# A decoder layer on one core: cross-attention's first maxima moved ahead of the residual work, mask probes and query splitting rearranged, key parts stored once

## The reference, cut to what matters

```python
x = x + self_attention(layernorm(x))        # 16 heads of 64, values rounded to fixed point
x = x + cross_attention(layernorm(x), ctx)  # 16 heads of 8, keys = values = ctx of 4 x 1601
x = x + mixture_of_experts(layernorm(x))    # 8 experts, 2 per token
```

## Time and profile before

| what | value |
|---|---|
| median of three runs | 664.87 us |
| the profiled execution | 664.56 us |
| its span in the trace | 662.8 us |
| busy in the span: TensorE, VectorE, ScalarE, POOL | 552.0, 496.2, 458.3, 140.1 us |
| granted TensorE clock, mean | 0.937 of full |
| bytes moved by DMA | 62.89 MB |

### The profile page before, as it was taken

The page is one execution under the profiler, slowest core; times in us unless marked ns, Lnnn a source line. Parts: engine busy times, 40 slices in busy tenths (PEclk is TensorE's granted clock), DMA queues, the critical chain, the costliest instruction groups (busy, mean ns, idle before and its releaser), DMA issues.

```text
span 662.8 us, 13915 instructions
## 1 busy us (share of the span) xinstructions
PE 552.0 (83%) x5115; PEld 303.4 (46%) x5115; DVE 496.2 (75%) x893; ACT 458.3 (69%) x815; POOL 140.1 (21%) x215
## 2 busy tenths in 40 slices
PE   5788897988777479989889998899989893899992
PEld 3455454545456233333333333233333232799992
DVE  3568889888986996888878887588878744576662
ACT  3888987898853046778678776577767873577750
POOL 5000001000003442230125010230001216222232
PEclk9999998999978779999999999699999987799995
DMA  9930953744766537010641018000000501111113
GB/s 227 251 115 6 194 214 107 160 153 138 217 155 194 89 112 243 2 52 1 144 133 51 2 40 205 32 1 2 2 2 4 191 6 51 40 41 42 42 29 103
DMA packets 31669, 62.89 MB, mean 95 GB/s; under 512 B 4526, under 2 KB 21338, under 8 KB 31156
## 3 DMA queue, kind: packets, MB, share of 16 engines
q0 software_dynamic: 8000, 40.91, 23.5%
q1 hardware_dynamic: 22020, 20.31, 10.5%
q10 hardware_dynamic: 1584, 0.79, 0.4%
HBM read 42.29 MB, written 19.30 MB: 93 GB/s over the span
## 4 chain that ended last, share of the span: by engine, by line
PE 45%; DVE 26%; issue 9%; ACT 9%; DMA 6%; SPq 2%; POOL 1%; DVEq 0%; POOLq 0%; ACTq 0%
DVE smax L1707 12%; PE pair L1102 11%; PE pair L1266 6%; PE pair L1077 6%; PE pair L1032 5%; DVE region_p L1570 4%; PE pair L1254 3%; ACT region_p L1346 3%; DVE region_p L1600 2%; ACT region_p L1434 2%; PE pair L930 2%; PE pair L1276 2%; PE pair L983 2%; DMA region_p<-nmT 1%; DMA region_b<-nmT 1%
## 5 line engine op out<-in xcount | busy, mean ns | idle before, releaser
L1434 ACT ACTIVATE region_p<-pair 128x1024 f32<-128x1024 f32 (+3 forms) x277 | 217.5, 811 | 70.9 <-PE pair L1077 65.5
L1707 DVE TENSOR_REDUCE smax<-pair 128x2 f32<-128x1024 f32 x192 | 225.7, 1219 | 48.5 <-PE pair L1032 47.6
L1570 DVE SCALAR_TENSOR_TENSOR region_p<-region_p 128x1024 int16<-128x1024 int16 (+1 forms) x56 | 68.2, 1219 | 9.8 <-ACT region_p L1332 7.8
L1102 PE MATMUL pair<-region_p,region_b 128*32 128x256 f32 (+1 forms) x832 | 68.7, 403 | 0.2 <-ACT region_p L1441 0.2
L1102 PE MATMUL pair<-region_p 128*32 128x256 f32 (+1 forms) x832 | 66.9, 395 | 0.5 <-ACT region_p L1441 0.4
L1077 PE MATMUL pair<-region_b,region_k 59*128 59x256 bf16 (+1 forms) x416 | 54.7, 273 | 8.5 <-ACT region_p L1434 3.9
L1032 PE MATMUL pair<-region_k,region_b 56*128 56x512 bf16 (+1 forms) x256 | 43.9, 360 | 15.5 <-DVE smax L1707 14.1
L1346 ACT ACTIVATE region_p<-region_p 128x256 f32<-128x256 int16 x128 | 51.6, 418 | 2.3 <-DVE region_p L1570 2.3
L1266 PE MATMUL pair<-region_p 128*128 128x128 f32 x368 | 45.7, 278 | 0.0
L1266 PEld LDWEIGHTS pair<-region_p 128*128 128x128 f32 x368 | 43.8, 195 | 0.0
L916 PE MATMUL pair<-identb,region_p 128*128 128x128 bf16 x256 | 20.6, 226 | 24.8 <-DVE region_p L1600 24.6
(11 more groups left out here) (249 smaller groups left out, 945.4 us busy)
## 6 DMA issues: line engine op xcount, KB each, us to landing
kimg<-region_k SPq DMA_DIRECT2D x56, 200.1 KB
region_k<-kimg POOLq DMA_DIRECT2D x8, 1400.9 KB, 16.7
region_b<-in_mask_Bx1xSxS_ff POOLq DMA_DIRECT2D x12, 800.5 KB, 6.9
region_p<-in_mask_Bx1xSxS_ff POOLq DMA_DIRECT2D x4, 800.5 KB, 13.1
region_k<-in_L_ffn_W POOLq DMA_DIRECT2D x3, 1024.0 KB, 8.4
xdisp<-region_x POOLq DMA_DIRECT2D x1, 2322.0 KB, 19.8
region_b<-in_ctx SPq DMA_DIRECT2D x3, 768.0 KB
xdisp<-region_x POOLq DMA_DIRECT2D x1, 2257.5 KB, 19.1
```

What stands on the lines that cost most here:

```text
L1102: last = pe.matmul(pair[3][32 * h:32 * h + 32, 512 + s % 2 * S:512 + (s % 2 + 1) * S], v_heads[b % 2][0:rows, t, c:c + 32], pT[0:rows, n / ...
L1434: act.activation(pT[0:rows, first // 3 % 2, k:k + size], home[0:rows, 0:size], ACT.Exp).then_inc(expt_made, 1)
L1570: return dve.scalar_tensor_tensor(out_, floor16, 0.0, floor16, ALU.is_lt, ALU.add)
L1707: last = dve.tensor_reduce(units[:, :, c // 3, c % 3], both, AX.X, ALU.max)
```

## The change

- **Probes.** In pairs 1 to 6 the two halves move from the ends of b = 0 and 1 to the ends of b = 2 and 3. Pair 7 is as before.
- **Keys.** The image keeps each part once: 6 stores a context instead of 14. A load names its source with a leading step of zero, so that one part fills 24 rows (three copies) or 16 (two): 3 DMAs for each half, 6 a batch instead of 2. POOL's loads for batch 1 wait until the queries of piece 0 are split.
- **Passage.** TensorE projects tiles 2 to 4 ahead of the first transposition and tile 5 behind it; tiles 6 and 7 come after chunks 0 and 1. VectorE does chunks 0 and 1 first; at chunk 2 it rounds, adds and takes statistics of all six later tiles together; variances follow at chunk 4, the inverse root at 5. POOL normalizes the six tiles and does the two subtractions of the split; ScalarE makes the seven copies. `QUERIES_AT` becomes 12, 14, 16.

The rest of the diff renames functions and renumbers semaphore counts (`layer_norm` is cut into `norm_stats`, `norm_var`, `norm_inverse`, `norm_apply`, with the same instructions).

```diff
+LATER = (S // 128, NT)
+KEY_ROWS = tuple((8 * min(p for p, (i, j) in enumerate(PRODUCTS) if j == part), sum(j == part for i, j in PRODUCTS)) for part in range(3))
-QUERIES_AT = (9, 11, 13)
+QUERIES_AT = (12, 14, 16)
+OUT_AT, VAR_AT, ROOT_AT = 2, 4, 5
-        kimg = nc.dram_tensor("kimg", (B, 128, HP, S2), BF16, kind="Internal").ap()
+        kimg = nc.dram_tensor("kimg", (B, 2, 3, 8, HP, S2), BF16, kind="Internal").ap()
...
-                for p, (i, j) in enumerate(PRODUCTS):
+                for j in range(3):
                     for a in range(2):
-                        sp.dma_start(kimg[CTX_ORDER[k], 64 * a + 8 * p:64 * a + 8 * p + 8, :, :].rearrange("d h k -> h d k"),
+                        sp.dma_start(kimg[CTX_ORDER[k], a, j, :, :, :].rearrange("d h k -> h d k"),
                                      kparts[64 * a:64 * a + 64, k % 2, j, :]).then_inc(kimg_written[k % 2], 16)
...
-                pool.dma_start(kstack[64 * a:64 * a + KROWS, b % 2, :, :],
-                               kimg[b, 64 * a:64 * a + KROWS, :, :]).then_inc(keys_loaded[b % 2], 16)
+                for j in range(3):
+                    first, count = KEY_ROWS[j]
+                    pool.dma_start(kstack[64 * a + first:64 * a + first + 8 * count, b % 2, :, :],
+                                   kimg[b, a, j, :, :, :].unsqueeze(0).broadcast_to([count, 8, HP, S2])).then_inc(keys_loaded[b % 2], 16)
...
             mask_load(0)
+            pool.wait_ge(qnat_made[0], 5)
             for k in range(2):
-                pool.wait_ge(kimg_written[k], 448)
+                pool.wait_ge(kimg_written[k], 192)
             for a in range(2):
                 keys_load(1, a)
...
-            chain.step(pool.tensor_copy(rows_of(0), xn_later))
-            chain.step(pool.tensor_tensor(xn_later, xn_later, rows_of(0), ALU.subtract))
-            pool.tensor_copy(rows_of(3), rows_of(0)).then_inc(qnat_made[1], 1)
...
+            pool.wait_ge(rstd_made, 1)
+            for t in range(*LATER):
+                last = pool.tensor_scalar(xn[:, t, :].rearrange("p (h a d) -> p a h d", a=2, d=XD),
+                                          x1[:, t, :].rearrange("p (a h d) -> p a h d", a=2, d=XD),
+                                          meanvar[:, t, 0:1], rstd[:, t:t + 1], ALU.subtract, ALU.mult)
+            last.then_inc(xn_made, 1)
+            pool.wait_ge(xn_made, 3)
+            for n, signal in enumerate((later_high, later_mid)):
+                pool.wait_ge(signal, 1)
+                pool.tensor_tensor(xn_later, xn_later, later_rows(n), ALU.subtract).then_inc(later_rest, 1)
+                pool.wait_ge(later_rest, n + 1)
             split_maxima(0)
...
-            project_out(1, (2, 4))
+            project_out(1, (2, 5))
...
             queries_T(0, pair[0])
-            project_out(1, (4, 6))
-            project_out(2, OUT_TILES[2])
+            project_out(1, (5, 6))
...
                 for p in range(LEAD):
+                    if p == OUT_AT:
+                        project_out(2, OUT_TILES[2])
                     pair_of_chunks(p, masked)
...
+            std_of(3, LATER)
+            act.wait_ge(xn_made, 3)
+            act.wait_ge(qpads_made, 2)
+            act.activation(later_rows(0), xn_later, ACT.Copy).then_inc(later_high, 1)
+            act.wait_ge(later_high, 1)
+            act.activation(later_rows(3), later_rows(0), ACT.Copy).then_inc(qnat_made[1], 1)
+            act.activation(later_rows(5), later_rows(0), ACT.Copy).then_inc(qnat_made[1], 1)
+            act.wait_ge(later_rest, 1)
+            act.activation(later_rows(1), xn_later, ACT.Copy).then_inc(later_mid, 1)
...
-                    if b < 2 and not first:
-                        mask_probe(*((HP - 1, 0) if last else (hp - 1, 1)), b)
+                    if b >= 2 and not first and not last:
+                        mask_probe(hp - 1, 1, b - 2)
+                    if b < 2 and last:
+                        mask_probe(HP - 1, 0, b)
...
+            def out_later(p):
+
+                if p == OUT_AT:
+                    out_floor(1)
+                    out_floor(2)
+                    dve.wait_ge(out_moved, 3)
+                    out_add(LATER, 2)
+                    norm_stats(x1, LATER)
+                if p == VAR_AT:
+                    norm_var(LATER).then_inc(var_made, 1)
+                if p == ROOT_AT:
+                    norm_inverse(3, LATER).then_inc(rstd_made, 1)
...
             for p in range(LEAD):
+                out_later(p)
                 pair_of_chunks(p)
```

More of the change, by code:

```diff
@@ L1212, in _ @@
                 last_finish()
-            xn_transposes(6, pair[2], FFN_TILES[1])
+            xn_transposes(5, pair[2], FFN_TILES[1])
             gates(1)
@@ L1546, in layer_norm, with norm_var @@
                 chain.step(last)
+            def norm_var(tiles):
                 for t in range(*tiles):
@@ L1566, in layer_norm, with norm_inverse @@
                 last.then_inc(xn_made, 1)
+            def norm_inverse(root, tiles):
+                dve.wait_ge(std_made, root)
+                return dve.reciprocal(rstd[:, slice(*tiles)], std[:, slice(*tiles)])
+            def layer_norm(n, root, src, tiles=(0, NT), meanwhile=None):
+                norm_stats(src, tiles)
+                norm_var(tiles).then_inc(var_made, 1)
+                if meanwhile:
+                    meanwhile()
+                chain.step(norm_inverse(root, tiles))
+                norm_apply(n, src, tiles)
             def truncate(out_, floor16):
@@ new lines, in out_add @@
+            def out_add(tiles, number):
+                first, end = tiles
+                cut_ = slice(first, end)
+                floor16 = qkv16[:, 0, 128 * first:128 * end].rearrange("p (t d) -> p t d", t=end - first)
+                chain.step(truncate(xn[:, cut_, :], floor16))
+                dve.scalar_tensor_tensor(x1[:, cut_, :], xn[:, cut_, :], 1.0 / FXP, x_in[:, cut_, :], ALU.mult,
+                                         ALU.add).then_inc(x1_made, 1)
+                dve.wait_ge(x1_made, number)
@@ L1676, in attention_out, with out_first @@
+            def out_first():
+                tiles = slice(*OUT_TILES[0])
+                out_floor(0)
+                dve.wait_ge(out_moved, 1)
+                out_add(OUT_TILES[0], 1)
+                layer_norm(2, 2, x1, OUT_TILES[0], lambda: make_o(HP - 1, B - 1))
                 xn_0 = xn[:, tiles, :].rearrange("p t (h a d) -> p (t h) a d", a=2, d=XD)
@@ L1855, in _ @@
                     dve.wait_ge(copies_made, 2)
-                    layer_norm(5, acc, FFN_TILES[0])
+                    norm_stats(acc, FFN_TILES[0])
+                    chain.step(norm_var(FFN_TILES[0]))
+                    norm_root(FFN_TILES[0])
+                    norm_apply(4, acc, FFN_TILES[0])
                     route(0)
@@ L1863, in _ @@
             dve.wait_ge(x2_made, B)
-            layer_norm(6, acc, FFN_TILES[1])
+            layer_norm(5, 4, acc, FFN_TILES[1])
             route(1)
```

87 lines of the change are left out of this document (34 added, 53 removed).

## The result

The kernel after took 674.17 us (median of four runs, 665.82 to 676.32) beside 664.01 for the kernel before on the same chip: ratio 1.0118, 95% interval 1.0061 to 1.0176. It is slower by about 1.2%; the forecast was 656.7. Its profiled execution took 675.21 us, its span is 671.7 beside 662.8 before.

The account below looks back on a forecast made before the run. No engine bounds the whole span: inside pairs three nearly level engines wait for each other, in the passage VectorE's rate ends up counting. Probes 6.3 plus passage 1.6, keys nothing, gave 664.6 - 7.9 = 656.7 us; range 650.5 to 663.2.

Parts of the forecast that it names:

- Probes, 6.3: Pairs 1 to 5: moving the probes to where VectorE waits saves 6.3 us in all.
- the 1.5 of an odd pair: Pairs 1, 3 and 5: both probes on the chain, up to 1.8 us leave it, 1.5 gained in each.
- the 0.9 of an even one: Pairs 2 and 4: only the first probe is on the chain, 0.9 us gained in each.
- The floor that I put under the period, 19.7: Pair 5: with TensorE at 18.2 us of work and VectorE 18.8, the lowest period assumed was 19.7 us.
- Passage, 1.6: Passage up to the end of the 22 maxima: ends at 248.0 instead of 249.6, gaining 1.6 us.
- The cast at 0.29: Head of the passage: POOL's index column issues later, so the slow cast loses its 2.0 us; gain 0.5 there.
- The middle: Passage, residuals to the narrow chunk: VectorE through at 225.8 instead of 229.36, 3.6 us gained.
- nearest to the clamp: POOL's normalizing of six tiles in the passage: 0.45 us a tile, 2.7 in all, bounds up to 0.8 each.
- rival B: Passage: slow POOL normalizing or ScalarE copies make batch 1's queries late and eat its gain; 658.8 us, chance 0.19.
- no time of their own: Key stores: the 32 removed of 56 are waited for only by POOL, so removing them changes nothing.
- The same bytes land, so I take the same time: Key loads of batch 2: six loads take the same 16 us as the two before.
- rival D: First chunk's wait for keys: broadcast loads run on few engines and land late; 676 us at 50 us loads, chance 0.08.

Follow-up runs that it names:

- e1: The kernel after with key stores, loads and awaited counts as before; probes and passage stay changed: 658.18 us, ratio 0.9913.
- e7: e1 with the six later tiles normalized by VectorE instead of POOL: 656.99 us, ratio 0.9864.
- e11: The kernel after with VectorE normalizing, and key loads of batches 2 and 3 cut by heads, second halves behind the next maxima transfer: 651.67 us, ratio 0.981.
- e2: The kernel before with only the keys changed: 676.06 us, ratio 1.0244.
- e13: The kernel after with the loads' repeat turned round, each row repeated in place of the whole part (keys in wrong rows): 675.26 us in one run.
- e4: The kernel after with the second half of the key loads for batches 2 and 3 held until the next maxima transfer: 662.76 us, ratio 0.9996.
- e3: The kernel after with 14 plain loads of 8 rows a batch in place of six repeating loads: 716.47 us, ratio 1.0799.
- e10: e7 with the next batch's mask tiles, in batches 1 and 2, loaded behind the next maxima transfer and clamped together: 652.81 us, ratio 0.983.

## Why the prediction was wrong

*Probes, 6.3: right in kind, too high.* 5.7 us in the pairs of the kernel after, 4.5 against a run at the same clock. No probe is on its chain in pairs 2, 3 and 5; pair 2 came at 20.89 (forecast near 20.7), pair 5 at 20.27 (19.7). The mis-sized term is the 1.5 of an odd pair; 0.9 to 1.1 came, and 0.7 for the 0.9 of an even one. I had counted the first probe in full, but the earlier trace rows has 0.25 us of it on the chain of pair 2, and pair 3 has the same:

```profile
100.49 0.25 DVE mask_hi L1619
```

With the second's 0.98 an odd pair gives 1.2 by that. The floor that I put under the period, 19.7, did not help: it was too low.

*Passage, 1.6: 2.0 measured, by errors that cancel.* The cast at 0.29, as forecast. The end of the 22 chunks, 239.36, is 246.7 on the old scale (plus the 7.4 gained until pair 5), forecast 248.0. The middle was 2.9 us better than I had it: TensorE is through tiles 6 and 7 at 208.0, 215.4 on the old scale (forecast 217.7), and POOL begins to normalize at 215.56, 222.9 there (forecast 225.8). TensorE's timeline after:

```profile
204.16 3.84 PE L994 MATMUL pair<-wpT,region_g 128*128 128x128 f32 x32
```

But POOL's normalizing took 0.78 a tile, the top of the bounds, and not the 0.45 "nearest to the clamp": 2.0 us more, and VectorE's wait was 4.3 and not 2.2. That is the sign given for rival B, though its time was not the outcome. That the two errors nearly cancel is luck. One more term, put at nothing, was wrong: that the 32 removed stores have "no time of their own" is false, as SP loads the rows of ones behind them. With the stores of before the shorter pairs would have met a wait of 3.6 us at the cast (e1, e7). Storing once, with its loads, is worth 2.1 us between the traces of e1 and after, 4.0 between e7 and e11, and in e2 the 2.0 of the other cast.

*Keys: the step that failed.* "The same bytes land, so I take the same time" held neither for the load (at the longest 23.4 us for 17.5 in batch 2, 23.1 for 18.7 in batch 3) nor for what depends on it. I had looked only for who waits for keys. The keys were in time at the first chunk, so rival D failed at the place that it named. Its mechanism was half right: the load did run too long, and turning the repeat round made it shorter (e13), but the six pieces together had 14 rows in flight, as many as the two loads before; they are spread out in time. Who paid was somebody else on the same engines: the 3-KB transfer of maxima, on another queue. The sum had no term for it, and it cost 14.4 us in two steps. e1 (undo), e2 (alone) and e4 (same loads, other time) show it from three sides, e3 by growing it. Why the load itself is longer is settled only as far as e13 goes.

*What would have told.* The chain before had it: a transfer of 4.12 us in group 9 where the others took 1.79, in a step of 26.07 for which e10 needs 19.9. 2.3 of these 6.2 us are the transfer, most of the rest the clock behind it (e10). That no room was left behind a load stood in the profile, and I costed a change to that load without asking what came next on the DMA engines.

*The range* ended at 663.2, with D left out at 0.08. D's price, 676, lies near the result by accident: it was worked out for another wait. As one rival with one place it had to carry all the chance of a longer load.

## What to carry to other kernels

A load that nobody waits for is not free: list what small transfers are due on the DMA engines while it runs, and how much room each has, before its shape is changed. Where a transfer on the path is already longer than its quiet length, the place has no room left; move the bulk behind it (e10, e11). And a removed store is worth what waits behind it on its queue: here the rows of ones, and through them POOL and a cast.

## What the runs showed of the hardware that I had not expected

A 3-KB transfer takes 1.8 us alone, 7 to 9 behind repeating loads and 22 to 26 behind loads of 8 rows, though it has another queue. TensorE, idle for 6.6 us, came back at a granted clock of 0.54 over the next ten: the transfer was 5.2 us longer, the step 8.25. Loads of the same 25.6-KB rows ran at 82 GB/s with 8 rows to a load, 105 in plain pieces of 24 and 16, 180 in pieces of 24 and 16 from a repeated source, 190 with 28 rows and 185 with 56. POOL needs 0.78 us for a 128-column normalization that VectorE does in 0.27.
